# Value products last in each step, and the dispatch's transfers in every second step, in two attention layers of a four-layer kernel

## The reference

```python
for l in range(4):
    xn = layernorm(x)
    x = x + attention_l(xn) + ffn_l(xn)
# layer 2 (the third): causal softmax attention, 16 heads of 8; router picks 1 of 8 experts
# layer 3 (the fourth): the same with a latent kv projection and rotary parts of 32 shared
#   by the heads; router picks 2 of 8 experts, and a shared expert is added
logits = where(causal, einsum('bhsd,bhtd->bhst', q, k) * scale, -inf)
out = einsum('bhst,bhtd->bhsd', softmax(logits), v)
```

## Time and profile before

| | |
|---|---|
| median of three executions | 2511.58 us (2503.85 to 2516.45) |
| the profiled execution | 2516.36 us |
| its span | 2514.2 us, 61783 instructions |
| TensorE matmuls busy, weight loads busy | 76%, 54% of the span |
| VectorE, ScalarE, GpSimd busy | 63%, 49%, 45% |
| mean granted clock of TensorE | 0.844 |
| third layer's attention, first subtraction to last | 1201.65 to 1597.46 us |
| fourth layer's attention, first subtraction to last | 1853.59 to 2285.59 us |

### The profile page before, as it was taken

One profiled execution on the slowest core, in us unless ns is written; L12 is line 12 of the kernel. 1 busy time (PEld: TensorE's weight loads), 2 busy tenths in 40 slices (PEclk: granted clock), 3 DMA queues, 4 the chain that ended last, 5 costly groups with the idle time before them and its releaser, 6 DMA issues.

```text
span 2514.2 us, 61783 instructions
## 1 busy us (share of the span) xinstructions
PE 1907.0 (76%) x21198; PEld 1363.1 (54%) x21199; DVE 1575.3 (63%) x3649; ACT 1221.9 (49%) x2607; POOL 1139.9 (45%) x921
## 2 busy tenths in 40 slices
PE   1553799999999788805888888683768787777998
PEld 0223466666667566604566666462535555555666
DVE  2236788787888788856444444475655555554774
ACT  0232577676777555501555555552235455554553
POOL 0003477675555233320775555342036775543551
PEclk9785799999999899955677776696777878988999
DMA  8900000011000011120111113021043333420223
GB/s 228 178 0 0 11 17 17 18 40 46 2 2 2 26 47 47 57 71 19 51 53 33 32 30 94 17 60 56 1 105 98 99 104 92 104 79 26 62 63 116
DMA packets 165195, 138.38 MB, mean 55 GB/s; under 512 B 17128, under 2 KB 151368, under 8 KB 164976
## 3 DMA queue, kind: packets, MB, share of 16 engines
q1 hardware_dynamic: 151312, 107.24, 17.2%
q0 software_dynamic: 11584, 23.91, 2.8%
q10 hardware_dynamic: 2080, 4.19, 0.5%
HBM read 57.84 MB, written 52.01 MB: 44 GB/s over the span
## 4 chain that ended last, share of the span: by engine, by line
PE 47%; DVE 20%; issue 11%; POOL 11%; ACT 8%; DMA 2%; DVEq 1%; SPq 1%; ACTq 0%; POOLq 0%
PE duo L1167 12%; PE mo L1167 9%; POOL v L768 7%; PE ob L1167 7%; PE misc L1167 7%; PE acc L1167 6%; PE pt L1167 3%; ACT v L1040 3%; DVE nmax L2288 2%; ACT v L1039 2%; DVE v L1973 2%; DVE region L2291 1%; DVE v L1965 1%; POOL rstd L736 1%; DVE stats L1795 1%
## 5 line engine op out<-in xcount | busy, mean ns | idle before, releaser
L768 POOL TENSOR_TENSOR v<-v 128x768 f16<-128x768 f32 x256 | 419.7, 1640 | 461.6 <-ACT v L1040 459.6
L763 POOL TENSOR_TENSOR v<-v 128x512 f16<-128x512 f32 x256 | 290.5, 1153 | 257.1 <-DVE region L2291 256.8
L790 POOL DMA_INDIRECT results<-probT,dest_no x202 | 217.2, 1075 | 329.8 <-ACT probT L822 289.3
L1167 PE MATMUL ob<-wm,v 128*128 128x9 f16 (+1 forms) x5856 | 257.4, 180 | 107.5 <-POOL v L768 86.3
L1167 PEld LDWEIGHTS ob<-wm,v 128*128 128x128 f16 x5856 | 215.3, 99 | 190.6 <-POOL v L768 93.7
L2180 DVE TENSOR_REDUCE nm<-duo 128x2 f16<-128x256 f32 x256 | 108.8, 425 | 294.8 <-PE duo L1167 294.7
L1039 ACT ACTIVATE v<-mo 128x384 f32<-128x384 f32 x352 | 174.3, 495 | 205.4 <-PE mo L1167 203.2
L1102 ACT ACTIVATE v<-mo 128x512 f32<-128x512 f32 x256 | 153.4, 599 | 157.7 <-PE mo L1167 157.7
L2288 DVE TENSOR_REDUCE nmax<-duo 128x2 f32<-128x512 f32 x256 | 164.9, 686 | 82.5 <-PE duo L1167 82.5
L1167 PE MATMUL duo<-kT,wm 128*128 128x256 f16 x1212 | 172.6, 279 | 56.0 <-DVE kT L1961 30.4
L1040 ACT ACTIVATE v<-mo 128x384 f16<-128x384 f32 x352 | 175.6, 499 | 0.0
(11 more groups left out here) (318 smaller groups left out, 4376.6 us busy)
## 6 DMA issues: line engine op xcount, KB each, us to landing
prob<-slot_rows SPq DMA_DIRECT2D x101, 130.0 KB, 2.2
head_rows<-v SPq DMA_DIRECT2D x96, 128.0 KB
load<-wm SPq DMA_DIRECT2D x32, 384.0 KB
qT<-results SPq DMA_DIRECT2D x40, 256.0 KB, 3.1
qT<-wm SPq DMA_DIRECT2D x16, 384.0 KB
slot_rows<-prob SPq DMA_DIRECT2D x4, 1300.0 KB, 19.4
slot_rows<-prob SPq DMA_DIRECT2D x4, 1235.0 KB, 19.7
kT<-head_rows SPq DMA_DIRECT2D x40, 96.0 KB
```

The source lines that it names most:

```text
L763: pool.tensor_tensor(p16[:, p % 2, h, 1, :], p32[:, h, :], p16[:, p % 2, h, 0, :], ALU.subtract)\
L768: pool.tensor_tensor(p16_2[:, p % 2, 1, :], p32_2[:, p % 2, :], p16_2[:, p % 2, 0, :], ALU.subtract)\
L790: pool.indirect_dma_start(out=results[layer], out_offset=bass.IndirectOffsetOnAxis(ap=dest_no[:, 2 * b + t:2 * b + t + 1], axis=0), in_=y_ ...
L1167: return pe.matmul(dst, lhsT, rhs, start=start, stop=stop)
```

## The change

In the third and fourth layers' attention alone, two things. TensorE's value products of step p - 1 go from ahead of the maxima to the end of the step, behind the maxima, the last chunk's output and the preparation; VectorE's scaling of finished outputs goes to the end of its step likewise. And GpSimd sends a tile of the dispatch in each odd step instead of in every step from the first: 32 tiles in the first 64 steps of the third layer, 64 in all 128 steps of the fourth. The number of instructions of each kind stays the same.

```diff
@@ -778,6 +778,8 @@
                         else:
                             pair_low(i, p)
                         n = i * STEPS + p
+                        if layer > 1:
+                            n = n // 2 if n % 2 else n_tiles
                         if n < n_tiles:
                             send_row_tile(layer, n // ALL, n % ALL)
@@ -1530,10 +1532,6 @@
                         at = rows_ahead(layer, p, more)
                         if at:
                             turn_maxima(i + at[0], at[1])
-                        if p >= 1:
-                            average(i, parity, p - 1)
-                        elif begun:
-                            average(i - 1, 1 - parity, STEPS - 1)
                         at = ahead(layer, p, more)
                         if at:
                             maxima(i + at[0], at[1])
@@ -1543,6 +1541,10 @@
                             out_proj(i - 1)
                         if more:
                             prepare(i + 1, p)
+                        if p >= 1:
+                            average(i, parity, p - 1)
+                        elif begun:
+                            average(i - 1, 1 - parity, STEPS - 1)
                     if not more:
                         average(i, parity, STEPS - 1)
                         turn_o(i)
@@ -2207,10 +2209,6 @@
                         at = rows_ahead(layer, p, more)
                         if at:
                             turn_rows(i + at[0], at[1])
-                        if p and p % 4 == 0:
-                            scale_o(i, p // 4 - 1)
-                        elif p == 0 and begun:
-                            scale_o(i - 1, 3)
                         at = ahead(layer, p, more)
                         if at:
                             maxima(i + at[0], at[1])
@@ -2218,6 +2216,10 @@
                             add(acc_full, x_made, i - 1, 0)
                         if more:
                             prepare(i + 1, 1 - parity, p)
+                        if p and p % 4 == 0:
+                            scale_o(i, p // 4 - 1)
+                        elif p == 0 and begun:
+                            scale_o(i - 1, 3)
                     if not more:
                         scale_o(i, 3)
                         add(acc_full, x_made, i, 0)
```

## The result

The changed kernel took 2406.98 us (median of 4 executions, 2404.53 to 2412.08) beside 2512.78 us of the kernel before (4 executions, 2503.85 to 2516.45): ratio 0.9587, 95% interval [0.9557, 0.9616], faster by 106 us. The forecast was 2441, its range 2400 to 2493.

A forecast was written before the change was run, and what follows sets the result against it. A ring of waits, not an engine, bounded the kernel. From the profiled 2516.4 us, third layer -46 (reorder -32, transfers -14) and fourth -24 gave 2446, as a median 2441; range 2400 to 2493, own range 2415 to 2468.

The forecast's parts named there:

- ring E, L, A, S: Third layer: exponentials (E), GpSimd's subtraction (L), value products (A), scores (S), 4.51 us per two steps at 2.4 GHz.
- lower level: Third layer at 1.2 GHz: TensorE's own work becomes the bound, a step falling from 3.01 to 2.75 us.
- The part of the preparation that vanishes in TensorE's wait: Third layer: five blocks preparing the next chunk each hide up to 0.6 us in TensorE's wait for the subtraction.
- I leave the shares of both levels as they are: Both layers: shares of time at 1.2 and 2.4 GHz stay unchanged; upper level about 40% third layer, 62% to 80% fourth.
- Rival 1: Third layer: the upper clock spreads through it; chunks of 37.9 instead of 49.4 us, total 2392; chance 0.17.
- they cost next to nothing: Third layer: with transfers in odd steps a pair needs 4.48 us, under 4.51; first two chunks gain 14 us.
- of this I keep 24: Fourth layer: sparser transfers bring its first four chunks to the later four's time, 27 us, of which 24 kept.
- The ring of four steps: Fourth layer: waits for the turned maxima and for GpSimd together, 10.05 us, 2.51 a step; reorder alone gains nothing.
- T to M: Fourth layer, even steps: from turns of maxima (T) to maxima (M), which wait for VectorE's copy, 0.87 us.
- the six steps of the rotary work: Fourth layer, steps 3 to 8: VectorE's rotary work is the bound; effect zero, between -1 and +1 us a chunk.
- Rival 2: Fourth layer: the lost cover of the turns decides; +10 without transfers, -1 instead of -24 with; total 2491; chance 0.13.
- the path of 7.34 us: Fourth layer: from an even step's value products across three steps, with a transfer behind an odd step's subtraction, 7.34 us.

The follow-up runs named there:

- run 9: The changed kernel once more, unchanged, as the base beside three later variants on the same chip: 2408.06 us, 0.9587 of the kernel before.
- run 7: The changed kernel, but third-layer value products stand right behind the maxima, ahead of the preparation: 2454.96 us, 0.9693 of the kernel before.
- run 1: The kernel before with TensorE's and VectorE's new order alone, transfers in every step as before: 2443.32 us, 0.9649.
- run 12: The changed kernel with an extra 192-column subtraction in each third-layer step on GpSimd, TensorE's program untouched: 2459.13 us, 0.9776 of the kernel before.
- run 2: The kernel before in its old order, with only the transfers moved to odd steps: 2545.43 us, 1.0051.
- run 3: The changed kernel, but the fourth layer keeps the old order; transfers sparse in both layers: 2461.89 us, 0.9723 of the kernel before.
- Run 6: The changed kernel, but value products ahead of the maxima in the fourth layer's steps 6 and 8: 2431.55 us, 0.9592 of the kernel before.
- Run 10: The kernel of run 4 again, beside run 9 on one chip: 2388.88 us, 0.9505 of the kernel before.
- run 4: The changed kernel with the fourth layer's transfers in even steps instead of odd ones: 2429.41 us, 0.9602 of the kernel before.
- run 11: The changed kernel with no fourth-layer transfers in steps 4 to 8, still 8 per chunk: 2413.39 us, 0.9592 of the kernel before.

## Why the prediction held, and where it didn't

**The bound and the reorder, third layer: right.** The ring E, L, A, S is what is left: forecast 4.51 us a pair at the upper level, read 4.59. At the lower level TensorE was to be the bound, with 5.5 us a pair; the one pair without transfers that lies wholly in it in run 9's profile (1458.03 to 1463.67) takes 5.64. The part of the preparation that vanishes in TensorE's wait was put at 3.0 us a chunk and is 2.7 to 3.6 (run 7). Where transfers run in each step, GpSimd's 2.83 is the bound (run 1).

**The clock: the step that failed.** "I leave the shares of both levels as they are" is what failed. The prediction's own sign of being wrong, a mean clock that moves by more than 0.1 in either stage, came true: 0.70 to 0.92 in the third layer. The forecast kept the shares of both levels, because a stretch at 0.5 has TensorE busy for 15.47 of 16 us. That row showed only that being busy doesn't bring the upper level; it says nothing of what a shorter ring does. After, the stretch of the same times (1343 to 1359, other steps) reads

```profile
1343.00:1359.00 16.00, 13.31 (x216) 9.88 (x215) 9.94 (x24) 11.38 (x29) 14.90 (x11) 0.95 0.17 43
```

with less busy time, more matmuls (216 against 160) and the upper level. Rival 1 had this: chunks of 37.9 against 37.3 to 41.2 measured, a chance of 0.17. The 42 us by which the third layer came out lower than forecast are mostly this: full upper level was priced at 96 - 46 = 50 us, and 43 of the missing 60 points came, an estimate of 36 us. The Trainium skill (TensorE: Matmul & The Clock Gate, Part 1: The HAM clock gate) has sustained activity release the upper clock and idling take it back; run 12 agrees in direction (0.93 to 0.75 by GpSimd's longer work, with TensorE's waits for it up from 27.8 to 45.9 us). The earlier trace rows do not speak against it: a matmul takes about twice as long at 0.5 (1.92 us against 1.05 for the block of eight), so the level itself makes TensorE look busy. By the number of matmuls the slower stretch did less, 160 against 216, which in part follows from the level too. The forecast read the busy share as if it stood apart from the level. What it is in the longer ring that makes the clock fall, no run here tells apart.

**The transfers: the second step that failed, in the other direction.** Forecast -14 in the third layer and -24 in the fourth, -38 together. Run 2 has +12 for them in the old order; in the new one run 1 has 0.9649 and the changed kernel 0.9641 or 0.9587, a gain of 2 to 16 us that chips blur.

In the third layer "they cost next to nothing" failed: 4.48 was held against a ring of 4.51. On run 1's chip the sparse chunks take 40.5 to 42.6 us (run 3) where chunks without transfers take 37.3, so four sparse ones cost as much (167.4 us) as two dense and two free ones (166.2). Most of that goes with the lower clock, 0.82 to 0.88 in these chunks and 1.00 in those of 37.3; the result's one sparse chunk at 1.00 takes 38.0.

The fourth layer's 57.8 against 51.0 us a chunk was an unfair comparison: the 51.0 averages in the last chunk, which prepares nothing and takes 39.9. The chunks between them take 55.2, 51.4 and 54.4, mean 53.7. So the price of dense transfers was 4.1 a chunk and not 6.8, and four chunks that lose half their transfers stand against four that now get some. The later chunks' price was put at 3 us ("of this I keep 24, because transfers now run through all eight and the rings are tight", of 27); in run 2 it was the whole gain and more.

**The fourth layer's reorder: wrong by two errors that partly cancel.** That the stage's -24 came near the measured -17.4 is luck: it was given to the transfers alone, and the order brought about all of it (run 1). The ring of four steps was worked out at 10.05 us, equal to the old pace, so nothing was expected. After, at the upper clock (order of time, from the value products of an even step to those of the even step four later; the view ends inside the last row):

```profile
2133.07 0.60 PE L1169 MATMUL ob<-wm,v 128*128 128x9 f16 x18
...
2135.59 0.59 PE L1169 MATMUL ob<-wm,v 128*128 128x9 f16 x18 [0.52 <-POOL v L768]
...
2140.40 0.61 PE L1169 MATMUL ob<-wm,v 128*128 128x9 f16 x18 [0.20 <-POOL v L768]
...
2141.52 0.27 PE L1169 MATMUL duo<-ident_h,nm 128*4 128x128 f16 x2
...
2142.39 0.49 PE L1169 MATMUL duo<-load 120*128 120x128 f16 x4 [0.60 <-DVE xnT L2176]
...
2142.94 0.22 PE L1169 MATMUL ob<-wm,v 128*128 128x9 f16 x3
```

2133.07 to 2140.40 is 7.33 (forecast 7.34), T to M 0.87 (forecast 0.87), 2140.40 to 2142.94 is 2.54 (2.71): 9.87 for four steps. The ring was sound. What was wrong is what it was compared with: 2.53 a step is the third layer's old pace at the upper level, while the fourth layer before took 29.14 / 10 = 2.9 in the ten plain steps, with a clock of 0.81 to 0.90 and transfers in half of its chunks. The gain is 3.3 us a chunk there, and run 3, without the reorder, takes 30.2 us for the same ten steps, so that the order by itself is worth some 4.

The second error is the six steps of the rotary work, put at zero. They take 25.3 us in run 3 and 27.4 to 28.3 in the changed kernel, so the order costs 2 to 3 us a chunk. In step 8 the maxima wait 4.89 us, against 2.97 in the earlier trace rows:

```profile
2114.16 1.64 POOL L768 TENSOR_TENSOR v<-v 128x768 f16<-128x768 f32 x1 [5.26 <-ACT v L1042]
2114.76 1.58 DVE L2125 TENSOR_TENSOR prob<-prob 128x512 f32<-128x512 f32 x1
...
2115.95 1.25 POOL L749 DMA_INDIRECT slot_rows<-xd,slot_no  x1 [0.15 <-issue]
2116.84 2.60 DVE L2130 TENSOR_TENSOR wm<-prob,wm 32x512 f16<-32x512 f32 x1
2117.23 1.65 POOL L768 TENSOR_TENSOR v<-v 128x768 f16<-128x768 f32 x1
2119.47 0.41 DVE L2176 CAST xnT<-duo 4x256 f16<-4x256 f32 x1
2120.02 0.80 PE L1169 MATMUL duo<-region,kT 120*128 120x128 f16 x4 [4.89 <-DVE xnT L2176]
```

The lost cover (A is behind this wait now) and VectorE's two sums, 1.58 and 2.60 us long, sit on the path together. Before, the same two sums took

```profile
2113.13 1.14 DVE L2123 TENSOR_TENSOR prob<-prob 128x512 f32<-128x512 f32 x1
2114.76 2.00 DVE L2128 TENSOR_TENSOR wm<-prob,wm 32x512 f16<-32x512 f32 x1
```

so 1.04 us of the 1.92 by which the wait grew is in them, and the rest is about the time that the value products took inside the wait. The clock falls in this wait too (a stretch inside it, and one from its last microsecond on):

```profile
2115.00:2118.00 3.00, 0.14 (x2) 0.00 (x0) 2.93 (x3) 1.50 (x4) 2.82 (x3) 1.00 0.29 90
2119.00:2125.00 6.00, 4.98 (x43) 4.39 (x44) 3.08 (x8) 1.27 (x3) 0.00 (x0) 0.50 0.01 3
```

In a chunk of the short form (run 9) the sums run in 0.86 and 0.68 us, and the maxima wait for 2.18:

```profile
1849.80 0.86 DVE L2125 TENSOR_TENSOR prob<-prob 128x512 f32<-128x512 f32 x1
1851.15 0.68 DVE L2130 TENSOR_TENSOR wm<-prob,wm 32x512 f16<-32x512 f32 x1
1852.42 0.49 PE L1169 MATMUL duo<-region,kT 120*128 120x128 f16 x4 [2.18 <-DVE xnT L2176]
```

What decides between the forms, no run here was made to tell. Run 6 gives the cover back and gains 14.1 us in the stage. Rival 2 had the mechanism in the wrong place: it charged the lost cover to the plain steps, where the ring hides it, and not to steps 6 and 8, where VectorE's queue is full.

**One thing the ring said and I didn't use.** In the path of 7.34 us the transfer counts because it stands behind a subtraction of odd number, whose successor is awaited by value products in an odd step, with no T to hide it. Behind even ones it delays the products that wait behind T and M anyway; the four steps then come down to GpSimd's own 2 x (2.83 + 1.65) = 8.96. Run 10 has 4.53 for a pair, 9.06 for four, and is the fastest kernel. This is argued and not shown: the same kernel on run 4's chip gained as much in the stage with pairs of 4.91 us and more.

**Bounds and the rest.** The last transfer stayed hidden, and the experts' stage isn't later by more than the 1.0 us of "everything else". The chance of 0.86 for faster was borne out. The median lies in the forecast's range, but outside what I had called its own range (2415 to 2468), and nearer to rival 1 (2392) than to the forecast (2441): the order alone (run 1: 0.9649) brings nearly all of the gain, where the forecast gave it -32 and the transfers -38. The total came closer than its parts, which is luck: the order was put some 55 us too small and the transfers 22 to 36 too large.

## What to carry to other kernels

When a ring of waits is made shorter, the clock's share is part of the answer: price the change at both levels, and don't rule the better one out by a busy share read at the lower: there the same matmuls take longer. In this case the better level deserved most of the chance. Before charging a load to the stretch that has it, compare with steps that do the same work, not with a mean that holds a chunk without preparation; and a load that is spread over more steps is not cheaper until a run shows it. In a ring that spans several steps, look which of them has a wait that hides something, and put the extra work behind that one.

## What the runs showed of the hardware

- In the third layer the mean granted clock was 0.70 before, 0.92 after, 0.75 in run 12 (ring made 0.62 us longer) and 0.90 in run 7. TensorE was busy for 87, 90, 87 and 87% of these stages, so the busy share does not put them in order.
- In step 8 of the fourth layer the clock went from 1.00 to 0.50 in a wait of TensorE of 4.89 us (2115 to 2120 above).
- VectorE's sum of 32x512 takes 0.68 us at its shortest and 2.60 with GpSimd at work (2116.84 above); it ended at 2119.44, 0.56 after the subtraction of 2117.23 had ended, and the subtraction kept its 1.65 us. The sum of 128x512 before it likewise ended 0.54 after the subtraction of 2114.16. The Trainium skill (SBUF — State Buffer, Who interferes with whom) has only the port pair of VectorE and GpSimd contend, as an exclusive lock; the trace agrees, in that both sums end behind the subtraction and the subtraction isn't longer. But the sum of 32x512 had begun 0.39 us ahead of its subtraction, while an indirect DMA ran on GpSimd; which of the two held it up isn't shown. VectorE's scaled products of 128x512, which read one operand from PSUM, kept 0.68 to 0.69 us.
- With these sums at 1059 ns on average instead of 1229 (runs 11 and 9) steps 3 to 8 took 27.0 us a chunk instead of 27.4.
- An indirect DMA occupies GpSimd for 0.98 to 1.25 us, with 0.15 ahead of it.
- Chips differ by 0.8% for the kernel before (2512.6 and 2533.6 us) and by 1.5% for the changed one (2407 and 2443).
